# Where the GpSimd engine puts its indirect scatters: one send per slot, and a scatter that waits for a remainder

## The reference

```python
h = tokens(x)                        # 64 patches of 28x28x3 by W, + b, a class token, * pos_embed: (128, 65, 128)
h = h + lstm(layernorm(h))           # 65 steps in order, hidden size 128, over a batch of 128
h = h + moe(layernorm(h))            # 16 experts, top 2 of the router's softmax:
# logits = xt @ router_w.T + router_b; gates = top-2 probabilities
# out += gate_e * (gelu(xt @ w1_e.T + b1_e) @ w2_e.T + b2_e),  d_model 128, d_ff 512
```

## Time and profile before

| what | value |
|---|---|
| median of three executions | 675.24 us |
| span of the profiled execution | 771.4 us |
| granted TensorE clock, mean | 0.957 |
| PE, PEld busy | 647.2 us (84%), 594.7 us (77%) |
| DVE busy | 562.3 us (73%) |
| ACT busy | 493.0 us (64%) |
| POOL busy | 413.1 us (54%) |
| DMA, mean | 184 GB/s |

### The profile page before, as it was taken

The page is one execution under the profiler, slowest core; times in us unless marked ns, Lnnn a source line. Parts: engine busy times, 40 slices in busy tenths (PEclk is TensorE's granted clock), DMA queues, the critical chain, the costliest instruction groups (busy, mean ns, idle before and its releaser), DMA issues.

```text
span 771.4 us, 24553 instructions
## 1 busy us (share of the span) xinstructions
PE 647.2 (84%) x7952; PEld 594.7 (77%) x7952; DVE 562.3 (73%) x1797; ACT 493.0 (64%) x1259; POOL 413.1 (54%) x446
## 2 busy tenths in 40 slices
PE   4999999999999999988877665878888787888870
PEld 4999999999999999888875554766666666666660
DVE  3877888888888888778886444756565756677777
ACT  4678876766667666554446343657666767777783
POOL 0243344777767666655656646545555555545552
PEclk9999999999999999999997767999999999999995
DMA  8987877888888887765522222344323234444555
GB/s 318 372 263 271 277 253 251 261 267 256 276 261 267 276 244 236 236 213 182 162 64 60 71 63 73 108 123 119 111 78 98 78 93 118 138 137 131 170 177 195
DMA packets 71895, 141.67 MB, mean 184 GB/s; under 512 B 13078, under 2 KB 55650, under 8 KB 63838
## 3 DMA queue, kind: packets, MB, share of 16 engines
q1 hardware_dynamic: 62128, 121.69, 50.1%
q0 software_dynamic: 9280, 17.21, 6.4%
q10 hardware_dynamic: 366, 1.21, 0.5%
HBM read 116.35 MB, written 25.66 MB: 184 GB/s over the span
## 4 chain that ended last, share of the span: by engine, by line
PE 25%; DVE 24%; another core or an unknown queue 13%; issue 13%; ACT 4%; POOL 3%; DMA 1%; POOLq 0%; ACTq 0%; DVEq 0%; SPq 0%
PE pair L1279 14%; DVE patches L1099 7%; PE pair L1434 3%; DVE patches L1121 2%; PE pair L1325 2%; POOL sent L1235 2%; ACT pair L680 2%; PE pair L1452 2%; PE pair L1289 1%; DVE patches L1114 1%; DVE h L1172 1%; DVE patches L1107 1%; DVE patches L1132 1%; DVE field L843 1%
## 5 line engine op out<-in xcount | busy, mean ns | idle before, releaser
L1257 POOL DMA_INDIRECT back<-patches x160 | 157.0, 981 | 150.6 <-DVE patches L1114 104.6
L680 ACT ACTIVATE pair<-pair,b1s 128x256 f32<-128x256 f32 x320 | 126.3, 448 | 110.4 <-remote 51.5
L1279 PE MATMUL pair<-field,patches 128*128 128x128 f32 (+1 forms) x1408 | 173.9, 280 | 8.9 <-DMA patches<-in_x 8.6
L1279 PEld LDWEIGHTS pair<-field,patches 128*128 128x128 f32 (+1 forms) x1408 | 164.6, 194 | 9.6 <-issue 8.6
L1235 POOL DMA_INDIRECT sent<-pay,slot_own x130 | 149.2, 1148 | 40.3 <-issue 38.2
L1434 PE MATMUL pair<-patches,ex_hi 128*128 128x256 f16 x640 | 119.4, 280 | 47.8 <-DVE patches L1099 23.8
L605 ACT ACTIVATE gate<-pair,lbias 128x128 f32<-128x128 f32 x260 | 74.4, 369 | 98.1 <-PE pair L1294 88.6
L1452 PE MATMUL pair<-ex_hi,patches 128*128 x1280 | 117.4, 225 | 8.3 <-issue 6.1
L1247 POOL TENSOR_TENSOR rstd<-veps,cst 128x2 f32<-128x2 f32 (+1 forms) x68 | 58.0, 853 | 107.2 <-DVE veps L800 106.6
L1107 DVE CAST patches<-pair 128x256 f16<-128x256 f32 x80 | 33.7, 422 | 109.6 <-remote 105.2
L1434 PEld LDWEIGHTS pair<-patches,ex_hi 128*128 x640 | 56.6, 99 | 72.8 <-issue 64.0
(11 more groups left out here) (150 smaller groups left out, 1257.7 us busy)
## 6 DMA issues: line engine op xcount, KB each, us to landing
patches<-in_x SPq DMA_DIRECT2D x62, 1152.0 KB
patches<-sent SPq DMA_DIRECT2D x80, 130.0 KB
field<-in_we SPq DMA_DIRECT2D x64, 128.0 KB
field<-back SPq DMA_DIRECT2D x10, 768.0 KB
patches<-in_b SPq DMA_DIRECT2D x80, 64.0 KB
field<-in_pos SPq DMA_DIRECT2D x65, 64.0 KB
out_tower<-h SPq DMA_DIRECT2D x10, 384.0 KB
back<-patches POOLq DMA_INDIRECT x160
```

The lines of the kernel that those rows point to most:

```text
L680: last = act.activation(up[:, cols], up[:, cols], ACT.Gelu, bias=b1s[:, bass.ds(e * FC + 2 * half + i, 1)], scale=1.0 / E_SCALE)
L1257: pool.indirect_dma_start(back, bass.IndirectOffsetOnAxis(ap=dsti[j % NO][:, k:k + 1], axis=0), yo[j % NO][:, k, :], None, bounds_check=2 ...
L1279: last = pe.matmul(bank_of, l, w_, start=(c == KS and k == 0), stop=(c == KS - 1 and k == 2))
```

## The change

Three edits. First, from slot 64 on a slot has room for one send in place of four, so the 23 sends that stood in slots 64 to 74 stand one each in slots 64 to 86. Second, sends beyond slot 64 leave `step` and are issued at the end of `step_b`, behind the slot's two scatters of a tile; the `power` of slot 65 so stands before the send. Since a tile's first choice and second choice now fall in different slots, every such send waits for its ids, tags and payload. Third, the second of a tile's two scatters to `back` waits for `hlo_done` of the tile two places on (the last tile at the end). The instructions are otherwise the same in kind and number: 130 sends and 160 scatters.

```diff
--- before.py
+++ after.py
@@ -388,7 +388,7 @@
                     first = routed(place(t)[0]) + 1
                     if first > n or room == 0:
                         n = max(first, n + 1)
-                        room = 2 if n < PIECES - TWICE else 3 if n < AHEAD else 4
+                        room = 2 if n < PIECES - TWICE else 3 if n < AHEAD else 1
                     slots.setdefault(n, []).append((t, choice))
                     room -= 1
             return slots
@@ -1224,11 +1224,16 @@
                                 rows_sent(pool, k - NP)
                         pool.tensor_copy(pay[:, a:a + m, HID:ROW], tag[:, STARTS[g]:STARTS[g + 1], :]
                                          ).then_inc(tagged, 1)
-                for i, (t, choice) in enumerate(sends.get(n, ())):
-                    if both and n > AHEAD and i == 1:
-                        power(n, both)
+                if both and n > AHEAD:
+                    power(n, both)
+                if n <= AHEAD:
+                    send(n)
+
+            def send(n):
+
+                for t, choice in sends.get(n, ()):
                     g, col = place(t)
-                    if choice == 0:
+                    if choice == 0 or n > AHEAD:
                         pool.wait_ge(ids_done, (g + 1))
                         through(pool, tagged, g)
                         through(pool, yn_done, t)
@@ -1236,9 +1241,6 @@
                         sent, bass.IndirectOffsetOnAxis(ap=slot_own[:, g % 4, choice, col:col + 1], axis=0),
                         pay[:, t % NP, :], None, bounds_check=E * CAP - 1, oob_is_err=False
                     ).then_inc(sent_done[t % NP], 16)
-                if both and n > AHEAD and len(sends.get(n, ())) < 2:
-                    power(n, both)
-
             def power(n, both):
 
                 pool.wait_ge(veps_done, normed(n))
@@ -1252,11 +1254,18 @@
                 j = n - 3
                 if 0 <= j <= TILES_B - 1:
                     through(pool, dst_done, j)
-                    through(pool, y_done, j)
                     for k in range(HALVES):
+                        if k == 0:
+                            through(pool, y_done, j)
+                        else:
+
+                            through(pool, hlo_done, min(j + 2, TILES_B - 1))
                         pool.indirect_dma_start(back, bass.IndirectOffsetOnAxis(ap=dsti[j % NO][:, k:k + 1], axis=0),
                                                 yo[j % NO][:, k, :], None, bounds_check=2 * TOKENS - 1,
                                                 oob_is_err=False).then_inc(y_out[j % NO], 16)
+
+                if n + AHEAD > AHEAD:
+                    send(n + AHEAD)
 
             slots(step, step_b, steps_first=True)
```

## The result

The changed kernel takes 676.91 us in the median of 20 executions, the kernel before 673.95 us in 20 beside them. The ratio is 1.0047, 95% interval [1.0029, 1.0065]: about 3.2 us slower, beyond the 0.3% that passes for no change.

The account below looks back on a forecast made before the run. It took no engine as full in the traced expert stage, but untraced PE at 2.9 to 3.1 us a tile, POOL nearly full. Sum: 675.2 + 0 + 0 + 0 + 0, given as 675.0 us; range 666 to 680.

Parts of the forecast that it names:

- The freezes: Expert stage: all engines stop after runs of scatters; taken as a tracing cost, 92 of 96.2 us, so untraced gain nothing.
- the rival that they are real untraced: Freezes beside the two runs partly exist untraced, so breaking the runs up gains 5 to 7 us: 669; chance 0.25.
- Sends spread: Slots 67 to 86, one send each: POOL 12 us late at slot 86, hidden by 12 buffers; 0, bounds −0.4 to +5 us.
- The first load of results: Slot 116: 5.5 us of cover from SP's load to ACT's use, so POOL 2 us late fits in; 0.
- this place and its mechanism as the rival: POOL becomes late where SP waits, at tile 32's load and slot 116: slower, 680; chance 0.20.
- its mark for the forecast: Sign in the changed kernel's trace: SP still issues the first load at slot 116 without waiting for a landing.
- a hold of GpSimd by DVE beside the remainder: Shared-port lock on a scatter running beside DVE's remainder: not seen, scatter still 0.97 us, so no term.
- `power` and the wait: Slot 65's `power` ahead of the send: gain 0 to 0.4 us; second scatter's wait for the remainder: 0 to +2; both taken 0.
- the sum's 0: All terms of the change added to 0 on 675.2 us, with a few tenths either way.

Follow-up runs that it names:

- late GpSimd: The kernel before plus two small GpSimd operations with unused results behind the scatters of each of slots 75 to 86: 680.82 us, ratio 1.0109 to the kernel before.
- three late: Changed kernel with its sends beyond slot 63 in slots 64 to 79, plus one small unused GpSimd instruction in each of slots 80 to 82: 677.17 us, ratio 1.0065.
- first load later: The changed kernel with SyncE's first load of results in slot 117 in place of 116: ratio 1.0059 to the kernel before.
- after: The changed kernel itself, first comparison and trace: 676.91 us, ratio 1.0047 to the kernel before.
- after again: The changed kernel, unchanged, measured and traced a second time: 677.03 us, ratio 1.0047 to the kernel before.
- spread only: The changed kernel without the second scatter's wait for the remainder: 677.06 us, ratio 1.0026 to the kernel before.
- ten more: The changed kernel without the wait for the remainder, plus one small GpSimd instruction in each of slots 4 to 13: ratio 1.0037 to the kernel before.
- before again: The kernel before, unchanged, traced a second time: 674.34 us, span 672.5 us.
- wait only: The kernel before with only the wait for the remainder added: ratio 1.0006 to the kernel before.
- behind only: The changed kernel without the wait for the remainder and with four sends a slot, still behind the scatters: 673.23 us, ratio 0.9992 to the kernel before.
- two a slot: The changed kernel without the wait for the remainder and with two sends a slot beyond slot 64, behind the scatters: ratio 1.0007 to the kernel before.
- four and wait: The changed kernel with four sends a slot again, keeping the order behind the scatters and the wait for the remainder: ratio 1.0012 to the kernel before.
- last send late: Four sends a slot behind the scatters, no wait for the remainder, with only the last send moved to slot 86: ratio 1.0017 to the kernel before.
- to 79: The changed kernel with its 23 sends behind slot 63 placed in slots 64 to 79 in place of 64 to 86: ratio 0.9998 to the kernel before.
- to 79, again: The changed kernel with those 23 sends in slots 64 to 79, run a second time: 674.27 us, ratio 1.0014 to the kernel before.

## Why the prediction was wrong

**The freezes: right on the time, wrong on the trace.** "So I take the freezes as a cost of tracing itself" holds in that they are no part of the time of 675 us, and so does the forecast from it, that breaking up the runs brings nothing untraced. But I took them for a cost of every traced execution and expected a span of "about 750 to 765": it was 673.4. They come in one traced execution of 17, and in none of the timed ones (the longest of the 20 of the kernel before is 680.05 us); what sets them off is open, and whether tracing has a part in it too. The time of the undisturbed stage, worked out as 237 us, is 243.3 (first scatter at 414.50, last at 657.77). The runs of "12 and 10 scatters" are runs of 12 and 10 indirect DMAs; each begins with a send. The rival that they are real untraced is refuted.

**Sends spread: the sum was fair.** Forecast 12 us late at slot 74 before and 12 at slot 86 after, 0.33 us regained a tile, about 2 us left at slot 116. Measured 13.9, 14.5, 0.41 a tile, and 3.0 us.

**The first load of results: this step failed.** I had "7.4 us of cover at 3.86 us a tile, 5.5 us at 2.89. A POOL 2 us late fits in. 0." This is wrong in two ways. First, it is the whole time from the load to ScalarE's use of it, and the load itself takes its share: 4.30 us in *late GpSimd*, 4.78 in *three late*, 6.17 in *first load later*, the three traces in which ScalarE waited for it. Of the 6.62 us in the changed kernel that leaves 0.45 to 2.3. Second, the one who waits first is SyncE, and behind its wait stands the load of tile 56. SyncE can go on at 564.05 in the changed kernel (2.17 us behind tile 55's load); with a landing 1.35 us after the issue that leaves room for 2.4 us of lateness, with the 3.34 us of *three late* for 0.4 us. So 3.0 us of lateness is 0.6 to 2.6 us too late, by how fast the scatter lands; in the changed kernel's two traces SyncE was held 0.6 us. The prediction did name this place and its mechanism as the rival, but with the wrong cover, and gave it 0.20; its mark for the forecast, a first load issued "without waiting for a landing", was not met.

What this hold costs the changed kernel its traces show only in part. Counted from the first drain, five traces of spread kernels (*after*, *after again*, *spread only*, *ten more*, *first load later*) and five of kernels in time by then (*before again*, *wait only*, *behind only*, *two a slot*, *four and wait*) are 0.08 us apart at tile 48, 0.40 at tile 52, 0.72 at tile 54, and about 1.2 us from tile 68 on. But three more traces in which SyncE wasn't held stand outside this choice: with *last send late* and the two *to 79* the unheld ones take 239.2 to 245.0 us to the last drain, the spread ones 240.6 to 242.0, so at the last drain nothing is told apart. Near slot 116 it is: from the drain of tile 48 to that of tile 54 it takes 18.65 to 19.13 us in three spread traces, 17.62 to 18.12 in all eight unheld ones. In two of the three (*after again*, *spread only*) PE waits for tile 56, 0.30 and 0.37 us; in the third, *first load later*, it waits for tile 57. *After again*:

```profile
570.97 0.44 PE L1417 MATMUL pair<-cst,patches 128*128 128x128 f32 x2 [0.30 <-DMA patches<-sent]
```

In the other two spread traces, *ten more* and the first one of the changed kernel, it takes 17.63 and 17.83 us and PE has no such wait. So the hold reaches PE in some executions and not in others.

**The end: a term that was missing.** Nothing in the sum or the rivals spoke of the last tiles. The 114th DMA behind the last send starts 1.5 or 2.2 us late. With the last send in slot 86 it is four tiles from the end, and the end is 6.46 to 6.47 us in all six traces that have it there, 5.19 to 5.24 in the ten others without freezes. That is +1.27 us, one scatter more behind DVE's addition. The prediction had looked for a hold of GpSimd by DVE beside the remainder (L1099) and found none; that holds in every trace, but beside the additions (L1183) there is one, and it gives the end its steps.

**The two together.** The medians' ratios of the five spread kernels are 1.0026 to 1.0059, 1.0043 in the mean: 2.9 us. The end has one experiment of its own (*last send late*, 1.2 us by the medians, 1.27 by the trace). By difference some 1.7 us are left for the lateness at slot 116. That lateness costs time is shown by the timed runs: *three late*, with a little more of it than the changed kernel, is 2.9 us slower than *to 79, again*, which differs from it in three small instructions alone. That it is 1.7 us in the changed kernel is not shown directly, and the 0.6 us that SyncE is held there is less than that. What holds the scatter is open as well; only its place is shown.

**`power` and the wait: right, within the intervals.** Taken at 0; *behind only* 0.9992 and *wait only* 1.0006 bear both out. In each of three pairs the kernel with the wait has the higher ratio (1.0006 against 1, 1.0012 against 0.9992, 1.0047 against 1.0026), never beyond the intervals, so a cost of up to 0.2% isn't excluded. In the trace the wait's 0.12 to 0.37 us is near the 0.19 that was worked out. The time, 676.9 against 675.0, lies in the range; but the kernel before took 673.95 in the same comparison, so the sum's 0 was 3 us off.

No version beat both kernels. The fastest, *behind only*, is level with the kernel before (0.9992 [0.9976, 1.0007]).

## What to carry to other kernels

Where a queue (SyncE's) waits for another's writes to land, the cover is counted to the next thing in that queue, not to the user of what is loaded, and a late issue has its landing time on top. The time from a load to its use is not cover either: the load's own time goes off it. When work of a nearly full engine is spread out, the recovery moves with it: before, GpSimd had 42 slots to regain 14 us, after, 30. And a trace that is longer than the timed runs by a seventh is traced again before anything is argued from its gaps.

## What the hardware did that I had not expected

- Two traced executions of one program had spans of 771.4 and 672.5 us. In the longer one all engines stop together beside runs of GpSimd's indirect DMAs; in the other, and in the 15 traces of the changed kernel and the variants, never.
- One indirect DMA starts late without any wait of the program: 1.50 us in the kernels without the wait for the remainder, 2.17 or 2.18 in those with it (counted from 0.30 us behind the DMA before it, or 0.85 behind what it waits for). Its number is that of the last send plus 114 in all 17 traces, ten instructions more don't move it, and it moved as forecast in two kernels made to move it. Number 113, the 114th of the program, is held too where its delay can be seen (1.3 to 1.7 us in six traces; 419.05 in the changed kernel). Why 114, and why it starts anew behind the last send, no run here shows.
- Beside DVE's additions of results (L1183) a scatter waits. Of the 2720 scatters in the 17 traces 58 last more than 1.1 us, up to 1.74, and 57 of them start while such an addition runs. Beside DVE's remainder (L1099) they last 0.97 us, as alone.
- Where no addition of DVE holds one, GpSimd issues such DMAs 1.28 us apart, however late it is. From the end of the issue to a waiting SyncE that goes on it takes 1.35 to 1.51 us in six traces and 3.34 us in one.
